# Edge layer 0 in one pass, its statistics from the message pass, all scatters ahead of it, and places in two halves

## The reference

```python
# message block
m_in = concatenate([h_node[src], h_node[dst], h_edge], axis=-1)
m = silu(m_in @ W1 + b1) @ W2 + b2
agg = segment_sum(m, dst)
# edge layers, l = 0, 1, 2
x = concatenate([h[src], e], axis=1) @ W1[l].T + b1[l]      # 256 channels, all edges
mu, var = mean(x, axis=0), var(x, axis=0)
x = relu((x - mu) * rsqrt(var + 1e-5) * gamma[l] + beta[l])
h = segment_sum(x @ W2[l].T + b2[l], dst)
if l < 2: h, e = relu(h), relu(e)
```

## Time and profile before

| | us |
|---|---|
| median of 3 runs | 3303.43 (3301.45 to 3308.19) |
| span of the profiled execution | 3301.0 |
| TensorE matmuls busy | 2649.1 (80%) |
| VectorE busy | 1984.1 (60%) |
| ScalarE busy | 1271.9 (39%) |
| GpSimd busy | 2154.0 (65%) |

### The profile page before, as it was taken

The page is one execution under the profiler, slowest core; times in us unless marked ns, Lnnn a source line. Parts: engine busy times, 40 slices in busy tenths (PEclk is TensorE's granted clock), DMA queues, the critical chain, the costliest instruction groups (busy, mean ns, idle before and its releaser), DMA issues. The chain is left out here.

```text
span 3301.0 us, 59411 instructions
## 1 busy us (share of the span) xinstructions
PE 2649.1 (80%) x14001; PEld 1764.8 (53%) x14001; DVE 1984.1 (60%) x3553; ACT 1271.9 (39%) x3069; POOL 2154.0 (65%) x2211
## 2 busy tenths in 40 slices
PE   5689895777767878888889998667779877677998
PEld 1234443556656557777766656445556555454444
DVE  6999694544444467777779847555554655555111
ACT  4777514333333456666667622111112211112111
POOL 1777776777777767777758747777755777774000
PEclk7799998777677899999989999999989999998999
DMA  2343455755665389999949745555534555555000
GB/s 98 104 108 107 150 183 151 207 165 166 165 170 161 106 295 317 331 321 321 325 156 327 277 135 171 153 158 154 158 103 149 170 156 156 157 156 179 23 1 20
DMA packets 305072, 570.42 MB, mean 173 GB/s; under 512 B 54465, under 2 KB 140406, under 8 KB 303510
## 3 DMA queue, kind: packets, MB, share of 16 engines
q1 hardware_dynamic: 204582, 299.39, 29.3%
q0 software_dynamic: 86528, 219.09, 22.4%
q10 hardware_dynamic: 13824, 50.34, 3.8%
HBM read 465.21 MB, written 103.66 MB: 172 GB/s over the span
## 5 line engine op out<-in xcount | busy, mean ns | idle before, releaser
L503 POOL DMA_INDIRECT region<-tab,region x624 | 602.7, 966 | 285.4 <-issue 202.4
L1037 PE MATMUL psum<-w_all,region 128*128 128x256 f32 x2496 | 642.6, 403 | 0.7 <-ACT region L2143 0.7
L2267 POOL DMA_INDIRECT by_tile<-stage,place x416 | 408.4, 982 | 197.5 <-issue 126.7
L1037 PEld LDWEIGHTS psum<-w_all,region 128*128 128x128 f32 x2496 | 489.2, 203 | 68.2 <-issue 2.1
L587 ACT COPY region<-psum 128x256 f32<-128x256 f32 (+1 forms) x420 | 143.1, 341 | 852.6 <-PE psum L580 852.6
L580 PE MATMUL psum<-region 128*64 128x256 f32 (+1 forms) x1664 | 222.0, 391 | 193.9 <-DVE region L1797 119.5
L503 POOL DMA_INDIRECT tN<-tab,region x312 | 300.1, 962 | 95.1 <-issue 94.2
L503 POOL DMA_INDIRECT tA<-tab,region x312 | 297.8, 954 | 95.1 <-issue 94.4
L1048 PE MATMUL psum<-region 128*128 128x256 f32 x1040 | 277.1, 414 | 79.8 <-DVE region L1677 79.5
L594 PEld LDWEIGHTS psum<-fold,region 128*128 128x128 f32 x1470 | 215.1, 206 | 152.6 <-issue 152.6
L594 PE MATMUL psum<-fold,region 128*128 128x64 f32 x1470 | 276.4, 309 | 0.0
(11 more groups left out here) (403 smaller groups left out, 4658.9 us busy)
## 6 DMA issues: line engine op xcount, KB each, us to landing
region<-e_t SPq DMA_DIRECT2D x416, 256.0 KB
region<-by_tile SPq DMA_DIRECT2D x131, 264.0 KB, 3.0
stage<-e_rows SPq DMA_DIRECT2D x208, 132.0 KB
pre_dram<-region ACTq DMA_DIRECT2D x48, 512.0 KB, 6.0
pre_dram<-tN ACTq DMA_DIRECT2D x48, 512.0 KB, 6.0
region<-pre_dram SPq DMA_DIRECT2D x48, 512.0 KB
tN<-pre_dram SPq DMA_DIRECT2D x48, 512.0 KB, 5.1
tA<-dst_row SPq DMA_DIRECT2D x78, 256.0 KB
```

The lines of the kernel that those rows point to most:

```text
L503: pool.indirect_dma_start(ring[j][:, c, at:at + width], None, table[:, :], bass.IndirectOffsetOnAxis(ap=idx[:, c:c + 1], axis=0)).then_inc ...
L1037: mm = pe.matmul(banks[:, 2 * (j % 2) + c // 2, (c % 2) * 256:(c % 2) * 256 + 256], e_ring[:, j % E_SLOTS, c * D:(c + 1) * D], W(f"ee{l}") ...
L2267: pool.indirect_dma_start(by_tile[:, :], bass.IndirectOffsetOnAxis(ap=place[:, 2 * q + c:2 * q + c + 1], axis=0), stage[:, k, c, :], None) ...
```

## The change

Four things change.

Places: computed in two halves of 208 columns. High and low parts of the bases are stacked in one operand (`base_both`), so a step is two matmuls instead of three and a copy of half the width; 50 steps in six banks instead of 25 in four. The first 104 pairs are scattered once the first half is there.

Scatters: all 208 pairs are scattered ahead of the message pass, 80 of them behind `irregular_set` instead of 60.

Message pass: the target table is split into bf16 parts once, in the norm ahead of the pass, and stored as `tgt_hi` and `tgt_low`; the casts and subtractions of each group go away. In their place the pass now runs the 130 units over the edge features without relu, for the statistics of layer 0 (`source_units` with `message_units`, two banks).

Edge layer 0: `two_passes` is gone; layer 0 takes `merged_pass` with the sums of the message pass, and runs the 130 units a second time, over the relu'd features, for layers 1 and 2 (`layer_units`, one bank). In both places a unit is now four matmuls of 128 columns with the node one-hot as weights and four of 129 with the edges as weights, and its result is added one unit later. `LAG` is 2, and the turned window has one slot. ScalarE no longer passes over layer 0's edges for their total, and GpSimd's one-hots are gone.

```diff
-LAG = 3
+LAG = 2
...
+PLACE_HALVES = (slice(0, NG * GC // 2), slice(NG * GC // 2, NG * GC))
+PLACE_SLOTS, TRIANGLES_AHEAD = 6, 3
+TOTALS_SET, BASES_SET = 5, 7
-PUT_ENDS = (0, 128, 188, PAIRS)
+PUT_ENDS = (0, 128, PAIRS)
...
+            def triangle(n):
+                half, t = divmod(n, N_TILES)
+                if n >= PLACE_SLOTS:
+                    pe.wait_ge(S["setup_to_pe"], BASES_SET + n - PLACE_SLOTS + 1)
+                pe.matmul(psum[:, n % PLACE_SLOTS, 0:NG * GC // 2], upper_h[:, :], masks[:, t, PLACE_HALVES[half]],
+                          start=True, stop=False)
...
-                pe.matmul(to, upper_h[:, :], masks[:, t, :], start=True, stop=False)
-                pe.matmul(to, tile, base_hi, start=False, stop=False)
-                pe.matmul(to, tile, base_lo, start=False, stop=True).then_inc(S["setup_to_dve"], 1)
+            for n in range(2 * N_TILES):
+                half, t = divmod(n, N_TILES)
+                pe.matmul(psum[:, n % PLACE_SLOTS, 0:NG * GC // 2], tile_both[0:WIN, t:t + 1].to_broadcast([WIN, D]),
+                          base_both[:, PLACE_HALVES[half]], start=False, stop=True).then_inc(S["setup_to_dve"], 1)
+                if n + TRIANGLES_AHEAD < 2 * N_TILES:
+                    triangle(n + TRIANGLES_AHEAD)
...
-                pe.wait_ge(S["tabd_cast"], T["tabd_cast"] + 3 * (g + 1))
                 for part, edges in chunks:
-                    pe.matmul(part, ohT_ring[:, j % 2, edges], tabd_parts[:, j % 2, 0, :], start=False, stop=False,
+                    pe.matmul(part, ohT_ring[:, j % 2, edges], tgt_ring[:, j % E_SLOTS, 0, :], start=False, stop=False,
...
+            def source_units(i, j, sums_ps):
+                for m in UNITS_AT[j]:
+                    u, to = i * 10 + m, sums_ps[m % len(sums_ps)]
+                    lane, edge = u_lane[:, m % 2, :, :], u_edge[:, m % 2, :, :]
+                    pe.wait_ge(S["u_made"], T["u_made"] + u + 1)
+                    pe.nop(nofuse=True)
+                    pe.wait_ge(S["u_taken"], T["u_taken"] + u + 1)
+                    pe.nop(nofuse=True)
+                    pe.wait_ge(S["u_add"], T["u_add"] + u + 2 - len(sums_ps))
+                    for c in range(GC):
+                        pe.matmul(to[:, 0:D], lane[:, c, :], edge[:, c, 0:D], start=(c == 0), stop=(c == GC - 1))
+                    for c in range(GC):
+                        mm = pe.matmul(to[:, D:2 * D + 1], edge[:, c, 0:D], edge[:, c, 0:D + 1], start=(c == 0), stop=(c == GC - 1))
+                    mm.then_inc(S["u_mm"], 1)
...
-                for c in range(GC):
-                    mm = pe.matmul(unit_ps(m), u_both[:, m % 2, c, D:2 * D], u_both[:, m % 2, c, :], start=(c == 0),
-                                   stop=(c == GC - 1))
-                mm.then_inc(S["u_mm"], 1)
...
             with pe.Fori(0, TRIPS - 1) as i:
                 for j in range(UNROLL):
                     edge1(i, j + 1)
                     scatter1(i, j)
+                    source_units(i, j, message_units)
...
+            def unit_add(u, m, at, sums, sums_ps):
+
+                to, of = sums[:, bass.ds(at, D)], sums_ps[(m + 1) % len(sums_ps)]
+                dve.wait_ge(S["u_mm"], T["u_mm"] + u)
+                dve.wait_ge(S["u_add"], T["u_add"] + u)
+                dve.tensor_tensor(to, to, of[:, 0:D], ALU.add)
+                dve.tensor_tensor(gram[:, 0:D + 1], gram[:, 0:D + 1], of[:, D:2 * D + 1], ALU.add).then_inc(S["u_add"], 1)
...
+            def units_step(i, j, places, sums, sums_ps, rows):
+                for m, at in zip(UNITS_AT[j], places):
+                    unit_add(i * 10 + m, m, at, sums, sums_ps)
+                    unit_prepare(i * 10 + m + 1, i, m + 1, rows)
...
-            put_rows(*PUT_ENDS[0:2])
+            put_rows(0, PAIRS // 2)
+            pool.wait_ge(S["tile_tables"], 2)
+            put_rows(PAIRS // 2, PUT_ENDS[1])
...
+            def store_parts(n, tiles):
+                sp.wait_ge(S["tgt_lo"], n + 1)
+                for table, of in ((tgt_hi, hi_rows), (tgt_low, low_rows)):
+                    sp.dma_start(table[tiles.start * D:tiles.stop * D, :].rearrange("(t p) f -> p t f", p=D), of[:, tiles, :]
+                                 ).then_inc(S["tgt_w"], 16)
...
             sp.wait_ge(S["table_w"], 16 * 8)
+            sp.wait_ge(S["tgt_w"], 16 * 8)
...
             for j in range(UNROLL):
                 load1(j, j)
+            for k in range(STAGES):
+                sp.wait_ge(S[f"put{k}"], 32 * PAIRS // STAGES)
+            sp.wait_ge(S["idx_all"], 32)
+            sp.wait_ge(S["tile_tables"], 3)
+            for m in range(U_ROWS):
+                load_unit(m, m, u_rows["msg"])
```

More of the change, by code:

```diff
@@ L1507, in norm_blocks @@
                 p = norm_plan(T, tables, degrees)
-                for step in range(N_BLOCKS + 7):
+                for step in range(N_BLOCKS + (11 if tables else 7)):
                     if degrees and ("out", step) in p:
@@ L1653, in dve_program, with unit_places, units_end @@
+            def unit_places(i, j):
+                return [unit_place(i * 10 + m) for m in UNITS_AT[j]]
+            def units_end(sums, sums_ps):
+                unit_add(UNITS, UNITS % 10, unit_place(UNITS), sums, sums_ps)
+                dve.wait_ge(S["u_add"], T["u_add"] + UNITS + 1)
+                dve.tensor_scalar(gram[:, 0:D], gram[:, 0:D], 0.5, None, ALU.mult).then_inc(S["sums_set"], 1)
+            dve.wait_ge(S["folded"], 2)
             dve.wait_ge(S["nrm_cent"], T["nrm_cent"])
@@ L2020, in norm_blocks @@
                         act.copy(tN[:, q, 0:D], rows_bank(k, tiles)).then_inc(S["turn_act"], 1)
+                    if tables and 0 <= step - 7 < N_BLOCKS:
+                        q, _ = quad(step - 7)
+                        act.wait_ge(S["turn_dve"], p["xd", step - 7].out[1])
+                        act.copy(hi_rows[:, q, :], tN[:, q, D:2 * D]).then_inc(S["tgt_hi"], 1)
+                    if tables and 0 <= step - 9 < N_BLOCKS:
+                        n, (q, tiles) = step - 9, quad(step - 9)
+                        act.wait_ge(S["tgt_rest"], n + 1)
+                        act.copy(low_rows[:, q, 0:D], rest_rows[:, n % 4, 0:tiles, :]).then_inc(S["tgt_mid"], 1)
                 count_norm(T)
@@ L2438, in sp_program @@
             count_norm(T)
-            stored = 0
+            def store_parts(n, tiles):
[3 more added lines that the diff above has]
+                                 ).then_inc(S["tgt_w"], 16)
+            stored, before = 0, None
             for n in (1, 3, 5, 6):
@@ L2489, in merged_pass @@
                     sp_load_e(sp, T, j, j)
-                sp_table(sp, T.turns("adadadadadada"), tab2, 2 * D)
+                sp_table(sp, T.turns("adadadadadada") if l else table_turns, tab2, 2 * D)
                 for j in range(UNROLL // 2, UNROLL):
                     sp_load_e(sp, T, j, j)
+                if not l:
+                    sp.wait_ge(S["pass_ready"], T["pass_ready"] + 1)
+                    sp.wait_ge(S["u_made"], T["u_made"])
+                    sp.wait_ge(S["u_taken"], T["u_taken"])
+                    for m in range(U_ROWS):
+                        load_unit(m, m, u_rows["edge"])
                 with sp.Fori(1, TRIPS) as i:
```

618 lines of the change are left out of this document (210 added, 408 removed).

## The result

The changed kernel takes 3419.5 us (median of 4, 3418.9 to 3419.9), the kernel before 3302.4 in the same comparison: ratio 1.0344, 95% interval 1.0331 to 1.0357. The forecast was 3271.5 us, with a range of 3230 to 3334: wrong in sign, and 85 us outside the range. The profiled execution has a span of 3418.3 us where before had 3301.0.

What follows compares the result with a forecast made beforehand. GpSimd was taken to pace every gather pass. Span 3301.0 + 41 (message pass) - 71 (layer 0 merged) - 2 (small ones) = 3269 us; with the median 2.4 above the span, 3271.5 us, range 3230 to 3334.

Steps and rivals of the forecast that it cites:

- The first scatter: Places in halves: 0.43 us a step moves the first scatter from 70.4 to 50.1 us, bounds 47 to 55.
- the first gather: Message pass: after all scatters and the table stores at 1.55 us each, gathers start at 606 us.
- The first sum: Message pass: VectorE's first sum moves from 589.61 to 634.8 us.
- The terms of TensorE: A unit takes 1.85 us; a group averages 4.76 us in the message pass, 3.43 + 2.31 before hand-over in layer 0.
- the shorter lag: Tails of four passes: one window sum fewer in each, 0.8 us each, 2 in all on the path.
- TensorE is the bound: Merged layer 0: 5.89 us a group on TensorE over GpSimd's 5.15, 665 us in all, saving 71.
- under 4: Message pass: VectorE's work per group stays under 4 us, so it is not the bound.
- the hand-over of two units in a group: Layer 0, one bank: the second unit waits for VectorE 26 times, 0.15 us a group.
- rival B: Layer 0: every unit waits for VectorE on the single bank, +62 us, 3334 us; chance 0.10.
- the forecast 1152: Message pass, paced by GpSimd: the next product starts at 1152 us instead of 1111.35, +41, bounds 1144 and 1207.
- rivals A: Message pass: TensorE becomes the bound through VectorE waits and lower clock, 3326 us, deciding from 5.29 us a group; chance 0.17.
- the sign that I named for "wrong": A message-pass period over 5.3 us a group, listed among the signs that would show the forecast wrong.

Runs made afterwards that it cites:

- e1: Changed kernel without VectorE's never-taken branch for wide groups in the message pass and layer 0; 3312.6 us, ratio 1.0022.
- e2: Changed kernel with 98 never-executed instructions ahead of VectorE's message-pass loop; 3336.3 us, ratio 1.0086.
- e9: Changed kernel with 168 never-executed instructions ahead of VectorE's message-pass loop; ratio 1.0011 on other chips. Reservation: no run tested the reading of four 128-instruction parts.
- e17: Changed kernel with VectorE's two loops each in two copies, target comparison on one input, double groups moved to first and fifth; 3288.1 us, ratio 0.9954.
- e4: Kernel before with 224 never-executed instructions inside VectorE's loop in layer 0's second pass; 3415.4 us, ratio 1.0332.
- e5: Changed kernel with 118 never-executed instructions ahead of VectorE's message-pass loop; 3335.6 us, ratio 1.0099.
- e6: On top of e5, VectorE's target comparison in the message pass reads one tensor and a number per partition; 3333.4 us, ratio 1.0088.

## Why the prediction was wrong, step by step

**What held.** The first scatter at 53.1 (bounds 47 to 55; a step costs 0.58 us and not 0.43, since the copy at half width takes 0.39). The last scatter at 593.8 (590), the first gather at 610.7 (606), with table stores of up to 3.7 us where I had 1.55 each. The first sum at 643.0 (634.8) has one wait that I had not seen: the units' rows are loaded behind those of eight groups on SyncE's queue, and VectorE stands for them ahead of its first comparison.

```profile
610.66 0.98 POOL L497 DMA_INDIRECT region<-tabs,region  x1 [15.93 <-issue]
...
641.33 0.75 DVE L1634 SCALAR_TENSOR_TENSOR deg_lane<-node_no,part,deg_lane 128x512 f32<-128x512 f32 x1 [5.39 <-DMA deg_lane<-by_tile]
...
642.99 0.69 DVE L1585 TENSOR_TENSOR region<-region,psum 128x512 f32<-128x512 f32 x1 [0.30 <-issue]
```

The terms of TensorE held, here read in e1: a unit takes 1.84 us (1.85 taken), a group of the message pass 4.24 us with one unit, a group of layer 0 5.17 with one, where 3.43 + 1.85 had been summed. Layer 1 is 2.3 us shorter, where 0.8 had been counted for the shorter lag.

**The step that failed.** In layer 0 "TensorE is the bound", over 95% busy and at full clock, and in the message pass GpSimd, with VectorE "under 4" us a group and so never in the way. The sum of a group has a term for each engine's operations and none for the jump at the trip's end: I counted VectorE's operations and left out its program. The change puts units, their register loads and their waits into a loop unrolled eightfold with a branch for wide groups in each group, and takes the body from 292 to 381 instructions in the message pass; in layer 0 a body of 334 takes over from two of 159 and 181. None of VectorE's loops in the kernel before stands at its jump back, and so no row stood behind the assumption that a longer loop costs only its operations. But its trace has one stop of the same kind, which I passed over: at 366.41 a forward jump over code that these inputs don't use (L1433), and then nothing on VectorE until 369.38.

```profile
365.80 0.06 DVE L1374 MEMSET small<- 128x1 f32 x1
369.38 0.38 DVE L1423 MEMSET small<- 128x1 f32 x12 [3.52 <-issue]
```

What the stops cost: in layer 0 758.1 - 675.3 = 82.8 us (after minus e2, where nothing else differs in this loop), 6.9 for each of 12 jumps; about half is the stop as it reaches TensorE (3.90 us in place of 0.57) and half the lower clock behind it (2.9 us over the next 28 matmuls). In the message pass 26 us, the difference between after and e1; this is net, as the gathers are shorter beside the stops (mean 1.016 us in after, 1.048 in e1).

The Trainium skill has this (Runtime: NRT & Kernel Launch, "Instruction fetch mechanics"): an engine's instruction store holds two blocks of 256 instructions, eight on TensorE, refilled in sequence, and a taken branch whose target lies outside waits for a transfer. The runs agree in the main: stops of 3 to 5 us, transfers on the instruction queue, none at bodies up to 292, none on TensorE with a body of 395 (1003 compiled), and one body of 334 with and without them by its place. They don't agree on the size of a block. The transfers here are of 8 KB, one for each 128 instructions of VectorE. And two whole blocks of 256 would make the compiled body of 318 stand over one stretch of 61 places, but it stands at 154, 179 and 10 (266 less 256), 112 apart. Four parts of 128, of which one is the next to come, give all that was measured, with the reservation made under e9. By this page the rival would have been named, though not priced.

**The second term.** With the stops gone (e1), layer 0 takes 676 us and not 665: the hand-over of two units in a group costs TensorE two pauses of 0.77 us and 0.57 at the trip's end, 0.26 us a group, where I had 0.15. That is rival B's mechanism at a fraction of its price; a second bank for these units wasn't tried.

**The third.** Also with the stops gone, the message pass is bound by GpSimd, as forecast, but at 5.41 us a group and not 5.15: 562.5 us for its 416 gathers. The gathers had been taken over at 0.98 us; e1's and then e17's, by group (busy us, mean ns, idle before):

```profile
L497 POOL DMA_INDIRECT region<-tabs,region x208 | 218.7, 1052 | 78.6 <-issue 77.4 <-PE psum L574 1.2
L497 POOL DMA_INDIRECT tN<-tabs,region x208 | 217.3, 1045 | 63.4 <-issue 61.3 <-PE psum L574 2.1
```

```profile
L498 POOL DMA_INDIRECT tN<-tabs,region x208 | 211.0, 1014 | 63.4 <-issue 62.8 <-PE psum L575 0.6
L498 POOL DMA_INDIRECT region<-tabs,region x208 | 210.9, 1014 | 79.2 <-issue 75.5 <-PE psum L575 3.7
```

0.065 us on each of 416 gathers is 27 us, and with the 5 of the first gather that is the distance from the forecast 1152 to e1's 1183.5. I had judged GpSimd by its own queue and not by what VectorE does beside it (last section).

**The sum again.** 3271.5 + 57 (message pass: 5 start, 26 gathers, 26 jumps) + 93 (layer 0: 83 jumps, 10 hand-over) - 2 (the update behind the message pass, 43.3 us for 45.7) = 3419.5.

"Slower" stood in rivals A and B, but each with a price (3326 and 3334) too small and a mechanism that isn't the one. The period that A decides by (5.29 us) was passed (44.4 us a trip of the message pass is 5.55 a group, at a clock of 0.94), so the sign that I named for "wrong" did show; its cause was not among my candidates.

## What to carry to other kernels

Count the instructions of an unrolled loop's body on each engine, not only its operations: branches that are never taken, register loads and waits count. For VectorE here a body of 292 (268 compiled) was free, 334 (318) depended on the place, and 381 (357) stood in all five. Where an engine goes silent at the end of each trip, look at the instruction queue's transfers on the page, and move a rarely taken branch out of the loop into a second copy of it. A stop of 3.6 us in the loop that TensorE bounds cost about twice that here (6.9 us), since the matmuls behind the pause ran at the lower clock.

## What the runs showed of the hardware that I had not expected

**Dead code has a price, and dead code can pay.** 224 instructions that are never executed cost 110 us inside a tight loop (e4; eight executed tests are in it, for which at most 10 us had been allowed), and 98 ahead of one save 83 (e2).

**A gather on GpSimd takes 0.94 us, or up to 1.45 when it begins just behind a comparison of two tensors on VectorE.** In e17, in order of time, both engines:

```profile
900.70 0.95 POOL L498 DMA_INDIRECT tN<-tabs,region  x1 [0.30 <-issue]
...
901.05 0.75 DVE L1637 SCALAR_TENSOR_TENSOR deg_lane<-node_no,part 128x512 f32<-128x512 f32 x1
...
904.32 0.74 DVE L1637 SCALAR_TENSOR_TENSOR deg_lane<-node_no,part,region 128x512 f32<-128x512 f32 x1
904.45 1.43 POOL L498 DMA_INDIRECT tN<-tabs,region  x1 [0.30 <-issue]
...
907.15 0.75 DVE L1637 SCALAR_TENSOR_TENSOR deg_lane<-node_no,part,tN 128x512 f32<-128x512 f32 x1
907.44 1.28 POOL L498 DMA_INDIRECT tN<-tabs,region  x1 [0.30 <-issue]
```

The comparison reads two tensors from SBUF. Where it starts 0.35 us after the gather, the gather takes 0.95; where it starts 0.13 or 0.29 ahead, 1.43 and 1.28. Counted over 690 to 1150 us: of the gathers that begin 0.1 to 0.4 us after such a start, 51 of 51 in e1, 41 of 41 in e17 and 18 of 18 in the kernel after are over 1.1 us; of all the others 37 of 289, 10 of 309 and 39 of 318. In e1 28 of the 37 begin so behind the target comparison (L1570), which has two inputs as well; in after it is 15 of the 39, and what lengthens the rest isn't known. That it is the second input and not the comparison the runs show too. Of the gathers 0.1 to 0.4 us behind the target comparison's start, 16 of 16 are long in the kernel before, 28 of 28 in e1 and 13 of 13 in e5, all with two inputs; with one input 1 of 11 in e6 and 2 of 29 in e17. The Trainium skill (SBUF — State Buffer, "Who interferes with whom") says that a VectorE instruction with two inputs in SBUF contends with a GpSimd instruction that reads SBUF; it adds, as inferred, that the writing of descriptors is not held by it. The counts agree with the first: a gather, which takes its indices from SBUF, is held. That it is the read of the indices that waits is not shown.
